# V evacuated straight into one of two attention operands, heads 17 columns apart, in a loop body of two batches

## The reference

```
q = x @ wq + x @ Aq @ Bq * 4;  k = x @ wk;  v = x @ wv + x @ Av @ Bv * 4
q, k = rope(q), rope(k)                          # split in 16 heads of 16
p = softmax(causal(q k^T / 4));  o = (p @ v) joined @ wo
x1 = layernorm(x + o)
h = butterfly_up(x1 @ W_exp + b_exp);  g = gelu(h + up_bias)
out = layernorm(x1 + butterfly_down(g) @ W_con + b_con + down_bias)
```

## Time and profile before

| | us |
|---|---|
| median of three executions | 1168.69 |
| the profiled execution | 1166.34 |
| its span in the profile | 1164.3 |
| TensorE matmul busy | 1057.2 |
| TensorE weight load busy | 783.8 |
| VectorE busy | 875.2 |
| ScalarE busy | 720.7 |
| GpSimd busy | 570.0 |

### The profile page before, as it was taken

How to read it: one execution, slowest core, us unless ns; L and a number is a source line. 1 busy time by engine, 2 the same in 40 slices (tenths; PEclk the granted TensorE clock), 3 DMA queues, 4 the chain that set the end, 5 groups by cost and what they waited for, 6 DMA issues and landing times.

```text
span 1164.3 us, 28776 instructions
## 1 busy us (share of the span) xinstructions
PE 1057.2 (91%) x8974; PEld 783.8 (67%) x8974; DVE 875.2 (75%) x1946; ACT 720.7 (62%) x1113; POOL 570.0 (49%) x567
## 2 busy tenths in 40 slices
PE   5577789999999999999999999999999999999876
PEld 4454456767677776767667776767677776767575
DVE  6589967777777877777777877788777877777354
ACT  2176648476675848476675848476675848475523
POOL 4342435556383745556383745546383745544311
PEclk9687889999999999999999999999999999998999
DMA  7765453645465574656465474656465474652111
GB/s 271 164 197 122 157 127 108 180 119 184 105 219 128 154 186 123 178 122 188 98 219 128 154 184 123 179 120 188 100 219 129 154 186 123 177 121 62 66 38 37
DMA packets 94984, 169.91 MB, mean 146 GB/s; under 512 B 14872, under 2 KB 36120, under 8 KB 94944
## 3 DMA queue, kind: packets, MB, share of 16 engines
q1 hardware_dynamic: 93888, 166.53, 51.9%
q10 hardware_dynamic: 832, 1.83, 0.4%
q0 software_dynamic: 224, 1.04, 0.2%
HBM read 92.28 MB, written 77.07 MB: 145 GB/s over the span
## 4 chain that ended last, share of the span: by engine, by line
PE 57%; ACT 14%; DVE 12%; issue 8%; DMA 5%; POOL 3%; SPq 1%; ACTq 0%; DVEq 0%; POOLq 0%
PE ps_m L626 20%; PE ps_m L746 8%; PE ps_m L780 7%; PE ps_m L755 5%; PE ps_m L674 5%; ACT pT L858 5%; PE ps_m L785 4%; PE ps_t L717 3%; DVE g_lo L468 3%; DVE m_raw L991 3%; ACT gact L931 2%; PE ps_m L703 2%; DVE x1T L1020 2%; POOL o_c L1155 2%; DMA r_b<-r_scr 1%
## 5 line engine op out<-in xcount | busy, mean ns | idle before, releaser
L858 ACT ACTIVATE pT<-ps_t 128x512 f32<-128x512 f32 x640 | 330.2, 603 | 271.9 <-PE ps_t L717 271.4
L1142 POOL TENSOR_SCALAR_AFFINE_SELECT pT<-pT 128x512 f32<-128x512 f32 (+1 forms) x320 | 188.7, 592 | 377.9 <-ACT pT L858 376.1
L991 DVE TENSOR_REDUCE m_raw<-ps_m 128x1 f32<-128x512 f32 (+2 forms) x768 | 338.4, 501 | 36.7 <-PE ps_m L703 36.2
L674 PE MATMUL ps_m<-k_st,q_st 48*128 48x512 f32 (+3 forms) x1024 | 154.6, 357 | 48.1 <-DMA k_st<-qk_scr 18.6
L746 PE MATMUL ps_m<-pT,v_aug 128*32 128x512 f32 (+3 forms) x2048 | 158.7, 452 | 8.5 <-DVE m_raw L991 3.2
L674 PEld LDWEIGHTS ps_m<-k_st,q_st 48*128 48x128 f32 x1024 | 87.9, 190 | 107.3 <-issue 56.9
L626 PE MATMUL ps_m<-x1T,w_hi 128*128 128x512 f32 x512 | 152.0, 404 | 1.6 <-ACT x1T L887 1.0
L717 PE MATMUL ps_t<-q_st,k_st 50*128 50x512 f32 (+3 forms) x1024 | 123.5, 348 | 3.3 <-DMA q_st<-m_scr 1.9
L746 PEld LDWEIGHTS ps_m<-pT,v_aug 128*32 128x32 f32 x2048 | 60.3, 113 | 88.1 <-issue 78.5
L626 PEld LDWEIGHTS ps_m<-x1T,w_hi 128*128 128x128 f32 x512 | 94.5, 190 | 25.8 <-issue 2.3
L703 PE MATMUL ps_m<-eye,maskb 64*128 64x128 bf16 (+1 forms) x1280 | 89.3, 215 | 0.0
(11 more groups left out here) (120 smaller groups left out, 2094.6 us busy)
## 6 DMA issues: line engine op xcount, KB each, us to landing
qk_scr<-rot_hi SPq DMA_DIRECT2D x62, 512.0 KB, 3.6
q_st<-qk_scr SPq DMA_DIRECT2D x128, 192.0 KB, 4.5
k_st<-qk_scr SPq DMA_DIRECT2D x128, 192.0 KB, 4.8
qk_scr<-rot SPq DMA_DIRECT2D x32, 512.0 KB, 4.2
o_scr<-o_raw SPq DMA_DIRECT2D x64, 256.0 KB, 3.5
r_b<-in_xT SPq DMA_DIRECT2D x17, 512.0 KB, 5.2
o_c<-o_scr SPq DMA_DIRECT2D x32, 256.0 KB
r_b<-r_scr SPq DMA_DIRECT2D x32, 256.0 KB
```

The costliest lines, as they stand in the source:

```text
L674: return pe.matmul(scores[r][:, off:off + (qt + 1) * P], q_st[rows, pr, qt * P:(qt + 1) * P], k_st[rows, pr, 0:(qt + 1) * P], start=start, ...
L858: act.activation(pT[:, slot, half * T:(half + 1) * T], ps_t[:, ST_BANK[2 * n + r], :], ACT.Exp, scale=SCALE).then_inc(exp_done, 1)
L991: ins = dve.tensor_reduce(m_raw[:, g % 2, r, u // 2, qt:qt + 1], scores[:, off:off + (qt + 1) * P], AX.X, ALU.max, negate=True)
L1142: pool.affine_select(out=v, in_=v, compare_op=ALU.is_ge, fill=0.0, base=0, pattern=pattern, channel_multiplier=-1).then_inc(mask_done, 1)
```

## The change

`v_new`, the step VC and the semaphore `vcopy` are gone. `v_aug` becomes two operands, one for even and one for odd batches, and in each of them a head takes VH = 17 columns: 16 of V and one of ones. PV still loads 32 columns for a head, so 15 of them are the next head's V, and VROW = 287 columns are kept for each tile so that the last head has 32 as well. ScalarE's evacuation of V writes straight into the operand of the batch's parity, in groups of 16 columns, 17 apart; it waits until PV of two batches before is done. PV waits for both evacuations of its batch. So that the parity is known when the code is written, the loop's body now holds two batches' lists and has 6 rounds.

```diff
+VH = DH + 1
+VROW = VH * H + DH - 1
...
             put("XRES", i - 1, 0)
-            put("VC", i)
...
-        v_new = sb("v_new", [P, NT, D])
-        v_aug = sb("v_aug", [P, NT, H, 2 * DH])
+        v_aug = sb("v_aug", [P, 2, NT, VROW])
...
+        def fixed(i):
+
+            return [(s, s[1] % 2) for s in steps(i, True)]
+
+        def looped(i, like):
+
+            return [(s, t[1] % 2) for s, t in zip(steps(i, False), steps(like, False))]
+
         def each(eng, one):
 
             for i in (-1, 0, 1, 2):
-                for s in steps(i, True):
-                    one(s)
-            with eng.Fori(3, B - 1) as i:
-                for s in steps(i, False):
-                    one(s)
+                for s, odd in fixed(i):
+                    one(s, odd)
+            with eng.Fori(3, B - 2, 2) as i:
+                for k in range(2):
+                    for s, odd in looped(i + k, 3 + k):
+                        one(s, odd)
...
                 elif kind == "PV":
-                    pe.wait_ge(vcopy, b + 1)
+                    pe.wait_ge(evac["V"], 2 * b + 2)
...
-                                           v_aug[:, kt, GH * n + j, :], src,
+                                           v_aug[:, odd, kt, VH * (GH * n + j):VH * (GH * n + j) + 2 * DH], src,
...
                 elif kind == "V":
                     act.wait_ge(done["V"], 2 * b + n + 1)
-                    wait(act, vcopy, b)
-                    act.activation(v_new[:, 2 * n:2 * n + 2, :].rearrange("p a c -> p (a c)"),
-                                   pm, ACT.Copy).then_inc(evac["V"], 1)
-                elif kind == "VC":
-                    wait(act, done["PV"], NG * b)
-                    act.wait_ge(evac["V"], 2 * b + 2)
+                    wait(act, done["PV"], NG * (b - 1))
                     act.wait_ge(pool_c, 1)
-                    act.activation(v_aug[:, :, :, 0:DH],
-                                   v_new[:, :, :].rearrange("p a (h d) -> p a h d", h=H), ACT.Copy)\
-                       .then_inc(vcopy, 1)
+                    heads = v_aug[:, odd, 2 * n:2 * n + 2, 0:VH * H].rearrange("p a (h d) -> p a h d", h=H)
+                    act.activation(heads[:, :, :, 0:DH], pm.rearrange("p (a h d) -> p a h d", a=2, h=H), ACT.Copy)\
+                       .then_inc(evac["V"], 1)
```

More of the change, by code:

```diff
@@ L401, in layer @@
         fill = [sem(f"fill{g}") for g in range(NG)]
-        vcopy = sem("vcopy")
         st6 = [sem("ln1_stats"), sem("ln2_stats")]
@@ L510, in _, with one @@
             sp.dma_start(b_out, bout_d.partition_broadcast(P)).then_inc(c_in, DMA)
-            def one(step):
+            def one(step, odd):
                 kind, b, n = step
@@ L818, in _ @@
             for i in (-1, 0, 1, 2):
-                for s in steps(i, True):
-                    one(s)
-            with pe.Fori(3, B - 1) as i:
+                for s, odd in fixed(i):
+                    one(s, odd)
+            with pe.Fori(3, B - 2, 2) as i:
                 for kind, b, n, r in SHARED[-2 * RING:]:
                     last[BANK[kind, n, r]] = (kind, b + i - 1, n, r)
-                for s in steps(i, False):
-                    one(s)
+                for k in range(2):
+                    for s, odd in looped(i + k, 3 + k):
+                        one(s, odd)
             for kind, b, n, r in SHARED[-2 * RING:]:
```

## The result

The changed kernel takes 1199.2 us (median; 1191.02 to 1202.28) against 1168.64; the ratio is 1.0249, 95% interval 1.0212 to 1.0285. The forecast was 1177 and the range ended at 1188. The sign and its cause, fetches at the backward branch, were as forecast; the size was not.

What follows compares the result with a forecast made beforehand. TensorE was taken as the bound, matmul busy 1057.2 of 1164.3 us. Terms: -6.6 (wait for V) + 0.1 (memset) + 15.0 (five branch fetches) = +8.5 on the 1168.69 median, giving 1177 us; range 1160 to 1188.

Steps and rivals of the forecast that it cites:

- the branches no longer find their code: TensorE's loop: the doubled body no longer fits its code store, so five backward branches wait for a packet, 15.0 us.
- The 256 instructions a packet: TensorE's instruction queue: 1537 matmuls and as many loads over 12 packets in the first 250 us, 256 a packet.
- Net 3.0 us: TensorE at each backward branch taken: a fetch of 3.3 us, 0.3 us of it hidden by queued work.
- Rival 2: Loop's backward branches: a cheap fetch, 1 to 1.6 us each, pays back the gain, 1169 us; chance 0.12.
- rival 3: Loop's backward branches: a dear fetch, up to 5.9 us landing, 5 x 5.6 = 28 us, 1190 us; chance 0.07.
- the 0.5 us are not given back: Chain from scores through g_lo and reciprocal to WO: moves forward with TensorE, so each batch's 0.5 us stays won.
- The gain of 6.6 us: TensorE's wait for V's eviction: gone once ScalarE's copy ahead of it goes, 6.6 us over the run.
- the V layout: Eviction writing heads 17 columns apart and PV's weights loaded 68 bytes apart: both taken to cost 0.
- The dear ends of both terms: V's eviction doubling to 1.2 us; PV's loads rising to 178 ns, 17 us, 4 us of it kept for the range.

Runs made afterwards that it cites:

- experiment 1: The kernel before with only its loop body doubled to two batches, old V and its copy kept: 1194.1 us, ratio 1.0249.
- experiment 4: The changed kernel with each engine told at the top of every round where its backward branch goes: 1170.8 us, ratio 1.0045.
- 11: Kernel before, two-batch body, TensorE work left out down to 1354 instructions a round; for the trace: branches take 0.208 us, no TensorE packets.
- 12: Kernel before, two-batch body, less TensorE work left out, 1864 instructions a round; for the trace: stalls as the changed kernel does, 43 TensorE packets.
- experiments 1 to 3: experiment 1, then all batches as straight code without hardware loop: changed kernel 1164.1 us (0.9973), kernel before 1163.9 us (0.9972).
- 7: Changed kernel as straight code, GpSimd's second sum of the second rotation left out in every batch but the first: 1159.1 us, ratio 0.9919.
- 8: Kernel before as straight code with the copy of V, the same GpSimd sum left out: 1166.9 us, ratio 0.9977.

## Why the prediction was wrong in size

**Right: the branches no longer find their code.** It was taken from the count of packets in the trace alone, with no run of such a case, and experiments 1, 4, 11 and 12 show it: size decides, and a hint removes it. The 256 instructions a packet came out right by luck: the matmuls and loads of the first 250 us give it, but with register and wait instructions there are 3214, 268 a packet. Between two packets of straight code it is 256 indeed (4097 instructions over the 16 packets from 47.8 to 311.3 us).

**Right in the main: the idle time of a branch.** "Net 3.0 us" was 3.2 in experiment 1 and 3.5 in the changed kernel. There is luck in it: no row showed the price, and I picked it between the landing times of other transfers. Rival 2 had measured the packets rightly, 1 us each (0.9 to 1.4 us behind the branches), but the branch stands for 3.3 to 3.9 us around one.

**Failed: "Net 3.0 us" as the whole price.** The step left out that TensorE comes back at the lower clock. In the loop before the clock never fell, and TensorE never stood for more than 1.1 us at once. Measured in experiment 1: 1.3 us more busy time and 0.8 us of other waits, 5.3 us a branch. The term was 26.5 us where I had 15.0, and rival 3 (28 us) came nearer, by another mechanism. This is the larger share of the miss.

**Failed: "the 0.5 us are not given back".** I followed the chain from the late scores to g_lo, the reciprocal and WO, rightly, and moved every link by 0.5 us with its length kept. The lengths were not fixed. What GpSimd does at that moment hardly moved (its sum starts 2.34 us behind the first scores, where it was 2.45), and g_lo now meets it. The gain of 6.6 us was 0 (experiments 1 to 3), and it is 6.8 us (2 to 11) once the sum is out of the way (7 and 8). So the forecast's sign came from the branches alone. The clue stood in the trace of before: the earlier trace rows merge two instructions of g_lo, 2.78 us together, and taken apart they are 1.21 and 1.65 us, of one shape; 0.57 us of the second lie beside GpSimd's mask (337.19 to 337.76 us).

```profile
L468 DVE TENSOR_TENSOR g_lo<-gact,x1T x32: 1211/1222/1654, 204.8 to 1148.8; 128x1024 fp32r<-128x1024 f32 x32
```

**Not failed: the V layout.** A load of PV takes 113 ns on average after and before; TensorE's matmul time in PV is 159.0 us against 158.7. The eviction in groups of 16 takes 0.60 us. The dear ends of both terms can go.

**Open.** 15.0 - 26.5 and -6.6 - 0 explain 18 of the 22 us between 1177 and 1199. The profiled executions are 30.3 us apart: 27.4 us in the five rounds, 4.4 us ahead of the first backward branch, and 1.5 us less behind the loop. At that first branch (380.93 us in the kernel before) experiment 4, with the same V, is 3.8 us late as well, and experiment 1, with the old V, 0.5 us. So in these executions the new V loses some 4 us ahead of that branch. What does it there was not tested.

## What to carry to other kernels

Before a loop body is made larger, count the engine's instructions in a round, register and wait instructions too, and look whether instruction packets flow in the loop: with none, the body fits, and twice the body may not. Price a stall of TensorE with its clock and the waits after it: here 5.3 us for 3.2 us of idle time. When an instruction moves in time, ask what else runs at its new place on the engines that it can collide with: two instructions of one shape and different lengths in the old trace tell of it.

## What the runs showed that I had not expected

- TensorE's code store kept a round of 1354 instructions and not one of 1864; a refetch holds the branch for 3.3 to 3.9 us, of which its first packet takes 0.9 to 1.4, and a hint cuts that to 0.36.
- VectorE, ScalarE, GpSimd and SyncE branched in 0.04 to 0.06 us in every kernel with a doubled body (up to 0.09 with the hint), with up to 426 instructions in a round, though their packets (q14) did flow.
- A VectorE subtraction of two SBUF operands makes no progress beside a GpSimd sum or mask that started before it: 1.08 us plus the overlap, within 0.02 us in all 504 of the study, or 1.21 us where that is more.
- Behind each of the ten stalls of the changed kernel and of experiment 1 (3.0 to 3.6 us idle), TensorE's granted clock was at the 1.2 GHz level for 3.4 to 6.8 us.
